# Preparing the feed-forward weights beside the first input projections, and keeping them in HBM

## What is computed

```
sa, ca, ga, sb, cb, gb = split(silu(c) @ w_mod)          # ga, gb kept at |.| >= 0.25
h = layernorm(x) * (1 + ca) + sa
x = x + ga * mamba(h)        # projections, convolution, scan of 1024 x 16 states, projection
h = layernorm(x) * (1 + cb) + sb
x = x + gb * ffn(h)          # ffn: q(silu(q(h) @ q(w_gate).T) * (q(h) @ q(w_up).T)) @ q(w_down).T
```

## Time and profile before

| | |
|---|---|
| median of 3 runs | 5692.8 us (5690.31 to 5702.46) |
| the profiled execution | 5697.24 us, span 5695.4 us |
| busy, share of the span | PE 86%, DVE 88%, POOL 70%, ACT 53% |
| granted TensorE clock, mean | 0.939 |
| scan loop, about 174 to 3866 us | DVE and POOL nearly always busy |
| weights stage, 3911 to 4071 us | DVE busy, clock 0.54 |
| feed-forward tiles, 4072 to 5695 us | PE busy 1597 of 1623 us |

### The profile page before, as it was taken

How to read it: one execution, slowest core, us unless ns; L and a number is a source line. 1 busy time by engine, 2 the same in 40 slices (tenths; PEclk the granted TensorE clock), 3 DMA queues, 4 the chain that set the end, 5 groups by cost and what they waited for, 6 DMA issues and landing times. The chain is left out here.

```text
span 5695.4 us, 76622 instructions
## 1 busy us (share of the span) xinstructions
PE 4878.5 (86%) x21894; PEld 3374.1 (59%) x21894; DVE 4986.4 (88%) x4382; ACT 3044.8 (53%) x6526; POOL 4001.5 (70%) x1946
## 2 busy tenths in 40 slices
PE   6689898798888978979879798854599999999999
PEld 3455555455555554545545555542488888888887
DVE  1799999999999999999999999996888888888887
ACT  1677777677777767777767777761211111111111
POOL 0899999999999999999999999993422222221221
PEclk8899999999999999989989999986799999999999
DMA  2455555554555546555555555542101011001000
GB/s 101 143 179 178 172 193 170 175 185 166 188 171 181 191 154 192 173 173 194 167 175 180 171 189 171 176 163 68 34 34 33 28 33 33 29 31 33 29 31 26
DMA packets 394604, 728.33 MB, mean 128 GB/s; under 512 B 44051, under 2 KB 44179, under 8 KB 394102
## 3 DMA queue, kind: packets, MB, share of 16 engines
q1 hardware_dynamic: 394230, 724.19, 39.1%
HBM read 689.41 MB, written 34.61 MB: 127 GB/s over the span
## 5 line engine op out<-in xcount | busy, mean ns | idle before, releaser
L551 POOL TENSOR_TENSOR slot<-du,b_row 128x1024 f32<-128x1024 f32 x1024 | 2404.3, 2376 | 48.6 <-PE y_ps L914 43.8
L806 DVE TENSOR_TENSOR_SCAN decay<-decay,state,slot 128x1024 f32<-128x1024 f32 x592 | 1389.2, 2347 | 52.0 <-ACT slot L723 50.6
L714 ACT ACTIVATE decay<-delta,rate 128x512 f32<-128x512 f32 x2048 | 1326.2, 679 | 33.4 <-issue 10.6
L914 PEld LDWEIGHTS y_ps<-ident,slot 128*128 128x128 f32 x8192 | 1009.0, 150 | 334.9 <-issue 215.6
L914 PE MATMUL y_ps<-ident,slot 128*128 128x128 f32 x8192 | 1098.2, 287 | 89.0 <-POOL slot L558 83.7
L558 POOL TENSOR_TENSOR slot<-slot,c_row 128x1024 f32<-128x1024 f32 x432 | 1024.6, 2372 | 76.4 <-ACT state L703 74.0
L806 DVE TENSOR_TENSOR_SCAN slot<-decay,state,slot 128x1024 f32<-128x1024 f32 x432 | 1011.9, 2342 | 72.2 <-ACT slot L723 70.3
L1266 POOL TENSOR_TENSOR hq<-hid,qinv 128x1408 f32<-128x1408 f32 x64 | 166.4, 2600 | 1238.3 <-DVE qinv L1293 1238.3
L856 PE MATMUL work_ps<-h_t,win 128*128 128x512 f32 x2048 | 995.0, 631 | 36.0 <-DVE delta L777 19.6
L812 DVE TENSOR_TENSOR slot<-decay,c_row 128x1024 f32<-128x1024 f32 x592 | 724.3, 1224 | 56.1 <-DVE decay L806 3.2
L1234 ACT ACTIVATE act_gate<-gate_ps 128x512 f32<-128x512 f32 (+1 forms) x192 | 108.2, 564 | 1119.6 <-PE gate_ps L1375 621.5
(11 more groups left out here) (193 smaller groups left out, 7537.8 us busy)
## 6 DMA issues: line engine op xcount, KB each, us to landing
b_row<-b_c_rows SPq DMA_DIRECT2D x1024, 256.0 KB, 3.8
c_row<-b_c_rows SPq DMA_DIRECT2D x1024, 256.0 KB, 3.7
win<-in_w_in SPq DMA_DIRECT2D x256, 256.0 KB, 4.4
xt<-in_x SPq DMA_DIRECT2D x16, 1024.0 KB, 7.3
xr<-in_x SPq DMA_DIRECT2D x64, 256.0 KB, 4.3
x_after_mamba<-xr SPq DMA_DIRECT2D x64, 256.0 KB, 4.2
xa<-x_after_mamba SPq DMA_DIRECT2D x64, 256.0 KB, 2.8
xres<-x_after_mamba SPq DMA_DIRECT2D x64, 256.0 KB, 2.7
```

The source lines that it names most:

```text
L551: pool.tensor_tensor(slot[:, u % SLOTS, :, :], du[:, p % 2, :, :], two(b_row[:, u % BC_RING, :]), ALU.mult).then_inc(S["ub_ready"], 1)
L714: act.activation(decay[u % 2][:, i, :], delta[:, p % 2, i, :], ACT.Exp, scale=rate[:, 2 * p + i, n:n + 1]).then_inc(S["decay_ready"], 1)
L806: dve.tensor_tensor_scan(d if u in DVE_C else h, d, h, state[:, 2 * p, n:n + 1], ALU.mult, ALU.add).then_inc(S["scan_done"], 1)
L914: op = pe.matmul(y_ps[i][:, s, :], slot[:, u % SLOTS, i, s * P:(s + 1) * P], ident[:, :], is_transpose=True, start=False, stop=(n == N - 1 ...
```

## The change

The quantisation of the feed-forward weights is taken out of the weights stage and put into chunk -1 of the mamba part, behind position 20, on DVE and POOL (`prepare`). The rows are regrouped: five groups with two blocks of 128 rows of gate and two of up (2048 columns), one with one of each (1024), four of down (1408). They lie in `slot`, which is free then, four groups at a time. `slot` is therefore allocated ahead of the setup, where POOL issues the loads of the first four groups behind the last modulation weights. The later loads and all stores are issued by POOL too. The quantised rows go to three tensors in HBM.

The rounding becomes one operation for the step (the exponent bits, with a second bit operation in the same instruction) and two that each take the maximum with the half step and add or subtract it. The step lies in the PSUM of `decay`, the maxima and the negated scales in that of `y_ps`; so ACT's first decay and PE's first sum wait for the preparation to have ended.

In the weights stage the groups are loaded from HBM into four buffers. PE turns a piece, ACT copies the high part, and DVE subtracts it from the PSUM for the low part; `minus`, `take_high` and ACT's second copy are gone. The first token tile is quantised, turned and split between the pieces. Sixty of the 64 statistics are worked out on DVE at the end of the mamba part.

The core of the diff:

```diff
+PREP_AT = 20
...
+    OVER_TWO, TO_STEP = 0x40800000, 0x0B400000
+    q_gate = nc.dram_tensor("gate_quantised", (F, DM), F32, kind="Internal").ap()
...
+    PREP = [[(w_gate, q_gate, 2 * i, 2, 0), (w_up, q_up, 2 * i, 2, 2 * DM)] for i in range(FT // 2)]
+    PREP += [[(w_gate, q_gate, FT - 1, 1, 0), (w_up, q_up, FT - 1, 1, DM)]]
+    PREP += [[(w_down, q_down, r, 1, 0)] for r in range(KT)]
+    PREP_RING = SLOTS // 2
...
+                        pool.wait_ge(mod_loaded[2], 16)
+                        for g in range(PREP_RING):
+                            prep_load(pool, g)
...
-            decay = [ps(f"decay{k}", [P, 2, T]) for k in range(2)]
+            decays_ps = ps("decays", [P, 2, 2, T])
+            decay = [decays_ps[:, k, :, :] for k in range(2)]
...
+                    sp.dma_start(gb_col[:, :], mod_rows[2, :].rearrange("(j p) -> p j", p=P),
+                                 allow_slow_non_contiguous=True).then_inc(gb_loaded, 16)
...
+                    def prepare():
+                        for g in range(len(PREP) + 1):
+                            if g < len(PREP):
+                                v = prep_rows(g)[:, 0:prep_width(g)]
+                                pool.wait_ge(prep_scales, 5 * g + 4)
+                                pool.tensor_tensor(blocks(v), blocks(v), spread(prep_inv[g % 2], prep_width(g) // QB),
+                                                   ALU.mult).then_inc(prep_scaled, 1)
+                            if g >= 1:
+                                r = g - 1
+                                v = prep_rows(r)[:, 0:prep_width(r)]
+                                pool.wait_ge(prep_scales, 5 * r + 5)
+                                pool.wait_ge(prep_rounded, r + 1)
+                                pool.tensor_tensor(blocks(v), blocks(v), spread(prep_scale[r % 3], prep_width(r) // QB),
+                                                   ALU.mult).then_inc(prep_quant, 1)
+                                pool.wait_ge(prep_quant, r + 1)
+                                for w, q, row, n, col in PREP[r]:
+                                    m = w.shape[1]
+                                    pool.dma_start(q[row * P:(row + n) * P, :].rearrange("(a p) d -> p a d", p=P),
+                                                   prep_rows(r)[:, col:col + n * m].rearrange("p (a d) -> p a d", a=n)).then_inc(prep_saved[r % PREP_RING], 16)
+                            if PREP_RING <= g + 2 < len(PREP):
+                                n = g + 2
+                                pool.wait_ge(prep_saved[n % PREP_RING], prep_count(n - PREP_RING))
+                                prep_load(pool, n)
+                        for g in range(len(PREP) - PREP_RING, len(PREP)):
+                            pool.wait_ge(prep_saved[g % PREP_RING], prep_count(g))
+
...
+                            if c.reg is None and c.off == -1 and pos == PREP_AT:
+                                prepare()
...
+                        if u == 0 and c.reg is None and c.off == 0:
+                            act.wait_ge(prep_rounded, len(PREP))
...
+                        scale, inv = prep_scale[g % 3][:, 0:nb], prep_inv[g % 2][:, 0:nb]
+                        peak, minus = y_ps[0][:, 0, 0:nb], y_ps[1][:, 0, 0:nb]
+                        dve.wait_ge(prep_loaded[g % PREP_RING], prep_count(g))
+                        chain(q_amax(dve, peak, prep_rows(g)[:, 0:prep_width(g)]), 1)
+                        wait(dve, prep_quant, g - 2)
+                        chain(q_scale(dve, scale, peak), 2)
+                        chain(dve.tensor_scalar(minus, scale, -NUDGE, None, ALU.mult), 3)
+                        chain(dve.reciprocal(inv, minus), 4)
+                        if PREP[g][0][0] is w_down:
+                            tile = PREP[g][0][2]
+                            dve.wait_ge(gb_loaded, 16)
+                            dve.tensor_scalar(scale, scale, gb_col[:, tile:tile + 1], None, ALU.mult).then_inc(prep_scales, 1)
+                        else:
+                            dve.sem_inc(prep_scales, 1)
...
+                        v = prep_rows(g)[:, 0:prep_width(g)]
+                        step = decays_ps[:, :, :, :].rearrange("p a b t -> p (a b t)")[:, 0:prep_width(g)]
+                        wait(dve, prep_rounded, g)
+                        dve.wait_ge(prep_scaled, g + 1)
+                        chain(dve.tensor_scalar(step.bitcast(I32), v.bitcast(I32), OVER_TWO, TO_STEP, ALU.bitwise_and, ALU.bitwise_or), 1)
+                        chain(dve.scalar_tensor_tensor(v, step, HALF_STEP, v, ALU.max, ALU.add), 2)
+                        dve.scalar_tensor_tensor(v, step, HALF_STEP, v, ALU.max, ALU.subtract).then_inc(prep_rounded, 1)
+
...
@@ -822,6 +964,12 @@
                                 times_c(pos, c)
                             for step, arg, cc in steps(DVE_STEPS, c, (pos, 1)):
                                 HAVE[step](arg, cc)
+                            if c.reg is None and c.off == -1 and pos == PREP_AT:
+                                prepare()
+                            if c.reg is None and c.off == CH and pos == 0:
+                                for s in range(TILES):
+                                    dve.wait_ge(x1_done[s], CH - 1)
+                                mean_of_x1(range((CH - 1) * TILES))
 
                     dve.memset(huge[:, :], 1e30).then_inc(S["cleared"], 1)
                     dve.tensor_copy(dt_parts[3 * R:, :], one[3 * R:DT_ROWS, :].to_broadcast((2, T))).then_inc(S["cleared"], 1)
...
+                            pe.wait_ge(prep_scales, 5 * len(PREP))
                         if n == 0:
...
+        GROUPS = [[(q_gate, "gate", r, 0), (q_up, "up", r, DM)] for r in range(FT)]
+        GROUPS += [[(q_down, "down", r, 0)] for r in range(KT)]
 
...
-                    wait(sp, over_scale, r - 1)
+                    if r >= 4:
+                        sp.wait_ge(w_turned, turned(r - 4))
                     for w, _, tile, col in members:
-                        sp.dma_start(wrow[r % 2][:, col:col + w.shape[1]],
-                                     w[tile * P:(tile + 1) * P, :]).then_inc(w_loaded[r % 2], 16)
+                        sp.dma_start(wrow[r % 4][:, col:col + w.shape[1]],
+                                     w[tile * P:(tile + 1) * P, :]).then_inc(w_loaded[r % 4], 16)
                     if r == 1:
+                        load_first_tiles()
...
-                        sp.dma_start(gate_col[:, :], mod_rows[2, :].rearrange("(j p) -> p j", p=P),
-                                     allow_slow_non_contiguous=True).then_inc(rows_loaded, 16)
-                        load_first_tiles()
-
...
+                for i, piece in enumerate(pieces):
+                    if i in between:
+                        between[i]()
+                    dve.wait_ge(w_hi, i + 1)
+                    dve.tensor_tensor(target(piece, 1), turn_w[i % 3][:, 0:piece[5], :], target(piece, 0).bitcast(F32),
+                                      ALU.subtract).then_inc(w_lo, 1)
+
+            def weights_tensor(pe, between):
+                for i, (r, col, _, _, _, n) in enumerate(pieces):
+                    if i in between:
+                        between[i]()
+                    pe.wait_ge(w_loaded[r % 4], loads(r))
                     wait(pe, w_lo, i - 2)
                     for a in range(n):
-                        op = pe.matmul(turn_ps[i % 3][:, a, :], wq[r % 2][:, col + a * P:col + (a + 1) * P], ident[:, :],
-                                       is_transpose=True, start=(a == 0), stop=False, skip_group_check=True)
+                        op = pe.transpose(turn_w[i % 3][:, a, :], wrow[r % 4][:, col + a * P:col + (a + 1) * P], ident[:, :])
                     op.then_inc(w_turned, 1)
...
-                for i in range(len(pieces) + 1):
-                    if i == len(pieces) - 6:
-                        act.wait_ge(ln_c, 5)
-                        norm_first_tiles()
-                    if i < len(pieces):
-                        act.wait_ge(w_turned, i + 1)
-                        act.activation(target(pieces[i], 0), turn_ps[i % 3][:, 0:pieces[i][5], :], ACT.Copy).then_inc(w_hi, 1)
-                    if i >= 1:
-                        act.wait_ge(w_rest, i)
-                        act.activation(target(pieces[i - 1], 1), turn_ps[(i - 1) % 3][:, 0:pieces[i - 1][5], :],
-                                       ACT.Copy).then_inc(w_lo, 1)
-
+                for i, piece in enumerate(pieces):
+                    if i in between:
+                        between[i]()
+                    act.wait_ge(w_turned, i + 1)
+                    act.activation(target(piece, 0), turn_w[i % 3][:, 0:piece[5], :], ACT.Copy).then_inc(w_hi, 1)
...
+                    weights_scalar(act, {4: norm_first, X_AT + 2: lambda: x_high(FIRST[0])})
...
+                    weights_vector(dve, {10: lambda: quantise_x(FIRST[0]), X_AT + 3: lambda: x_low(FIRST[0])})
...
```

(2 more changed lines are left out.)

## The result

The changed kernel takes 5563.57 us (median of 4 runs, 5561.50 to 5566.19); the kernel before, on the same chip, 5692.80. The ratio is 0.977, with a 95% interval of 0.9753 to 0.9787: 129 us less. The profiled execution has a span of 5561.9 us, against 5695.4.

A forecast was written before the change was run, and what follows sets the result against it. DVE and POOL were taken to bound the scan loop, with all 160 us of the weights stage on the path. Terms -117.8 + 0.8 + 2.5 = -114.5 us, from 5692.8, gave 5578 us; range 5567 to 5601.

The forecast's parts named there:

- -117.8 + 0.8 + 2.5 = -114.5 us: Whole kernel: weights stage saves 117.8 us, moved statistics add 0.8, late preparation adds 2.5; forecast 5578 us.
- the worked total: Weights stage: 3.4 + 28.9 + 6.3 + 2.0 + 1.7 = 42.3 us instead of 160.1, saving 117.8.
- a weights stage that waits for DMA: Weights stage: waiting for DMA there was named as a sign that the forecast is wrong; no size given.
- DVE's 0.69 for a floor: Weights stage: DVE's subtraction allows no less than 0.69 us per piece; 0.85 was taken, 28.9 us for 34 pieces.
- The rival of loads as the pace: Weights stage: loads at 172 GB/s set the pace, 57.4 us, +15 us, 5593 us in all; chance 0.07.
- The sixty statistics: End of the scan loop: 4.05 us of statistics moved ahead of the last gate on DVE, 3.27 free; adds 0.8 us.
- I count no blocking: Preparation at the start: DVE's full passes have an operand in PSUM, so POOL's multiplications beside them cost nothing.
- The delay goes through whole: First scan: DVE ends the preparation 2.5 us late, and all of it reaches the total.
- An expensive issue on POOL: Preparation: 2.27 us per DMA issue on POOL, 20 us late instead of 2.5, 5596 us; chance 0.12.
- a full block: Preparation: DVE and POOL block each other, times add to 210.4 us, 54 late, 5630 us; chance 0.06.
- the slower case: Preparation: POOL's issues alone set its length, slower than before from about 6.8 us each, 5720 us at 8; chance 0.04.
- The better case (5570): Weights stage at DVE's floor of 0.69 us per piece and no overrun of the preparation: 5570 us; chance 0.05.

The follow-up runs named there:

- e3: Kernel before with gate_col allocated behind neg_mr1, so xa to hh lie as in the changed kernel: 5681.78 us against 5698.99 on the same chip, ratio 0.9971.
- e1: Changed kernel with one idle 128x4 tile between shift_row and xa, so all tiles from xa on lie 32 bytes higher: 5586.23 us, ratio 0.9802 to the kernel before.
- e11: Changed kernel with all 64 bn_aggr statistics in the weights stage again, as before: 5562.22 us, ratio 0.9769 to the kernel before.
- e12: Changed kernel with the down groups' scale written to and read from PSUM, and the first four groups' loads issued first in the weights stage: 5560.40 us, ratio 0.9764.
- e4: Changed kernel without the preparation and its loads, the weights stage reading the unquantised inputs directly: 5570.09 us, ratio 0.9775 to the kernel before.

## Why the prediction was wrong

**The step that failed** is the sum itself: "-117.8 + 0.8 + 2.5 = -114.5 us". It has no term for the feed-forward tiles, whose 1624 us were taken over from the kernel before without a word, because the diff leaves their code as it is. The diff does remove a tile of 16 bytes ahead of `hx` and `hh`, and that alone is worth 17 us (e3), 18 when it is undone (e1). With 2 us from the higher granted clock at their start, it makes up the missing term, 19.4 us by the two profiles. With it the sum would have given about 5559, 5 below what was measured; without it the error was 14.7. The 5 are about what the profiled execution of the kernel before lies above its median, 4.4.

**The weights stage** came out at the worked total, 42.8 us for 42.3 and 117.3 saved for 117.8, but not by the worked parts. The first turn came 3.2 us behind the stage's start (3.4 forecast), the tile's quantisation took 5.2 (6.3), and from the last turn to the first gate matmul it took 1.9 (1.7). Loads that came late cost 6.1 where the sum has nothing; the prediction itself named a weights stage that waits for DMA as a sign that the forecast is wrong. What is left for the 34 pieces and the operations slipped in between is 26.4 us instead of 28.9 + 2.0: the sum held PE at the lower clock through the stage and DVE's 0.69 for a floor, but the granted clock rose, four transposes went from 1.06 to 0.63 us, and the subtractions started 0.60 apart. These errors cancelled. The rival of loads as the pace was right about single groups and wrong about the stage, which moved 250 GB/s.

**The sixty statistics.** They stand in one run of 4.04 us from 3869.00, as forecast, and the `gate` behind them is at 3874.86 against 3871.22, 3.6 later, of which the end of the last scan accounts for 2.7: 0.9 for the 0.8 forecast. What the prediction had not seen is that keeping them in the stage would have cost nothing that can be measured (e11).

**The preparation.** The passes at 2.29, 1.62 and 1.22 us and POOL's multiplications at 3.68 and 2.58 are as in the sum. The waits for loads are 3.23, 2.09, 2.83 and 2.11 us, together 10.3 for 10.1, though POOL's issues cost 0.53 to 0.77 and not 1.0. Against that, its loads landed later: 704 KB in 6.0 us (median of four), beside its saves, instead of 4.2. The step "I count no blocking" held for the full passes and failed for one short operation: L910 has both ends in SBUF and cost 4.8 us more, so DVE was 7.5 us late and not 2.5. With that operation reading PSUM (e12) it is 2.65 late. "The delay goes through whole" isn't borne out either: 8.6 us at the first scan were 2.7 at the last, though such a difference of two profiles scatters by several us (e4). Both errors cancelled, and the stage began 3.2 us later where 3.3 had been forecast. That agreement is luck; in the variants with the same preparation and the same code up to there the stage begins 1.2 to 8.3 us later than in the kernel before.

**The rivals.** An expensive issue on POOL, a full block and the slower case are ruled out by the rows of DVE and POOL above. The better case (5570) had the right sign, but its reasons do not give the time: the pieces did fall below 0.85 us, the late loads took that back, and the preparation did overrun.

## What to carry to other kernels

When an edit adds or removes a tile, list the addresses of all the tiles behind it, and let a stage that "isn't touched" have a term in the sum; where TensorE is the bound with fp32r matmuls like these, try each stationary operand a multiple of 256 bytes away from the moving one that streams while it is loaded; it was worth 0.3% here. A short operation between two SBUF tiles on VectorE can be held for as long as a long one of POOL takes: look at every operation beside POOL's, not only at the full passes. A forecast that meets the total of a stage has not shown its parts: compare each term with its row. A delay at the front of a long loop isn't worth its size at the end until traces show it there, and one pair of them is too few where equal code ends 10 us apart.

## What the runs showed of the hardware

- Matmuls of 512 columns of fp32r follow each other every 226.6 to 226.8 ns when the stationary operand, loaded meanwhile, lies at a multiple of 256 bytes from the moving one, and every 232.8 to 233.4 ns with 32, 64 or 128 bytes more; both at a granted clock of 1.00. Of 384 columns: 173.2 to 174.0 at 0 and 32 bytes, 176.1 to 176.8 at 64 and 128. Offsets between these, and other strides, weren't run. Why it is so no row shows; that each weight load stands beside the matmul before it in the trace fits with a conflict of the two reads, but does not show it.
- Half of what faster matmuls gave per tile (0.50 us) was missing in the time of a tile, which fell by 0.25; the stretch with the wait for DVE's `hh_lo` behind the transposes grew by 0.15 us.
- A `tensor_scalar` of 88 columns between SBUF tiles took 0.27 us alone and 2.7 to 3.7 when a multiplication of POOL started 0.05 to 1.03 us after it, and ended with that one; one of 64 columns took 0.20 alone and 0.96 behind the start of one. With its source in PSUM it took 0.31.
- Subtractions of 512 columns on DVE, each shown with 0.68 or 0.69 us, started 0.60 us apart where nothing held them.
- A DMA issued by POOL cost 0.53 to 0.59 us of its time for one block of rows and 0.72 to 0.77 for two.
